# Split x kept once in DRAM: sixteen-row, four-step loads in the recurrence of a four-layer network

## What is computed

```python
xr, gate = jnp.split(x @ W_in.T, 2, axis=-1)          # inner width 1024
xr = xr + t_emb[:, None, :]
xc = silu(causal_conv4(xr, W_conv) + b_conv)
xn = (xc - mu) / jnp.sqrt(var + 1e-05) * ln_g + ln_b
Bm, Cm, dt = jnp.split(xn @ W_xproj.T, 3, axis=-1)    # 16 states
dt = jnp.tanh(dt @ W_dt.T + b_dt) * 0.01
Ad = 1.0 + dt * A
Bd = Bm * jnp.minimum(jnp.linalg.norm(xn, axis=-1, keepdims=True), 1.0)
def step(h, inputs):
    ad, bd, xt, ct = inputs
    h = jnp.clip(h * ad[:, :, None] + bd[:, :, None] * xt[:, None, :], -10.0, 10.0)
    return (h, jnp.einsum('bd,bdh->bh', ct, h))
y = ys + D * xn
out = x + y * silu(gate) @ W_out.T
```

## Time and profile before

| | us |
|---|---|
| median of 3 runs | 3763.84 (3762.84 to 3764.57) |
| the profiled execution | 3766.1, of which the span from first to last instruction is 3764.3 |
| PE busy | 3412.0 (91%) |
| DVE busy | 2965.0 (79%) |
| POOL busy | 1868.6 (50%) |
| ACT busy | 1355.2 (36%) |
| SyncE's DMA queue (q1) | 615.49 MB, 46.6% of 16 engines' time |

### The profile page before, as it was taken

One profiled execution on the slowest core, in us unless ns is written; L12 is line 12 of the kernel. 1 busy time (PEld: TensorE's weight loads), 2 busy tenths in 40 slices (PEclk: granted clock), 3 DMA queues, 4 the chain that ended last, 5 costly groups with the idle time before them and its releaser, 6 DMA issues. The chain is left out here.

```text
span 3764.3 us, 62060 instructions
## 1 busy us (share of the span) xinstructions
PE 3412.0 (91%) x22068; PEld 2260.9 (60%) x22068; DVE 2965.0 (79%) x3172; ACT 1355.2 (36%) x2078; POOL 1868.6 (50%) x1384
## 2 busy tenths in 40 slices
PE   7999839999996899999999999997999948999998
PEld 6777614444443667777777777775777733444444
DVE  4777769999996777777778777763576769999998
ACT  3555512221222553444444444432455522122121
POOL 2555645655563024444454444433355655556554
PEclk9999959999998899999999999998999968999999
DMA  4566765565554224222322222224466675555553
GB/s 128 217 259 257 271 239 203 203 219 214 200 215 142 80 72 138 85 82 78 111 96 87 80 83 85 74 63 133 162 259 237 257 294 196 217 201 210 216 206 136
DMA packets 288573, 631.00 MB, mean 168 GB/s; under 512 B 33472, under 2 KB 35904, under 8 KB 288224
## 3 DMA queue, kind: packets, MB, share of 16 engines
q1 hardware_dynamic: 281200, 615.49, 46.6%
q10 hardware_dynamic: 7104, 11.81, 0.9%
HBM read 390.75 MB, written 241.70 MB: 168 GB/s over the span
## 5 line engine op out<-in xcount | busy, mean ns | idle before, releaser
L1196 DVE CUSTOM_DVE_ANT_0 l0r_g<-l0r_g,l0r_pv,l0r_cf 128x1024 f32<-128x1024 f32 x512 | 641.9, 1336 | 20.6 <-PE l0r_pv L1005 19.0
L1196 DVE CUSTOM_DVE_ANT_0 l3r_g<-l3r_g,l3r_pv,l3r_cf 128x1024 f32<-128x1024 f32 x512 | 641.8, 1337 | 17.8 <-PE l3r_pv L1005 16.2
L137 PE MATMUL l1h_ps_p<-l1h_xh,l1c_wh 128*128 128x512 f32 x768 | 323.3, 421 | 5.6 <-issue 3.3
L139 PE MATMUL l1h_ps_p<-l1h_xl,l1c_wh 128*128 128x512 f32 x768 | 306.3, 399 | 0.0
L138 PE MATMUL l1h_ps_p<-l1h_xh,l1c_wl 128*128 128x512 f32 x768 | 304.9, 397 | 0.0
L2182 POOL TENSOR_TENSOR l1h_st<-l1h_veps 128x1 f32<-128x1 f32 x64 | 35.4, 554 | 530.5 <-DVE l1h_veps L2040 530.5
L1794 ACT ACTIVATE l1h_pt<-l1h_ps_t 128x512 f32<-128x512 f32 x256 | 151.4, 591 | 330.7 <-PE l1h_ps_t L1667 330.7
L1020 PE MATMUL l0r_py<-l0r_g,l0r_cd 128*32 128x512 f32 x2048 | 253.1, 613 | 1.3 <-ACT l0r_y L1105 1.3
L1020 PE MATMUL l3r_py<-l3r_g,l3r_cd 128*32 128x512 f32 x2048 | 252.0, 611 | 0.8 <-ACT l3r_y L1105 0.8
L2080 DVE TENSOR_TENSOR l1h_e<-l1h_e,l1h_mx 128x1024 f32<-128x1024 f32 x128 | 207.2, 1619 | 4.4
L2099 DVE TENSOR_TENSOR l1h_vt<-l1h_ps_p,l1c_dc 128x512 f32<-128x512 f32 x64 | 44.3, 691 | 194.6 <-PE l1h_ps_p L139 194.6
(11 more groups left out here) (400 smaller groups left out, 8965.1 us busy)
## 6 DMA issues: line engine op xcount, KB each, us to landing
l0r_x<-xhl_s SPq DMA_DIRECT2D x128, 512.0 KB, 5.9
l3r_x<-xhl_s SPq DMA_DIRECT2D x128, 512.0 KB, 5.7
xhl_s<-l0a_xo SPq DMA_DIRECT2D x116, 512.0 KB, 4.6
xhl_s<-l3a_xo SPq DMA_DIRECT2D x116, 512.0 KB, 4.6
gate_s<-l0a_gate SPq DMA_DIRECT2D x64, 256.0 KB, 3.0
l0r_dx<-dx_s SPq DMA_DIRECT2D x32, 512.0 KB, 7.7
l0r_gate<-gate_s SPq DMA_DIRECT2D x32, 512.0 KB, 8.6
l0r_crow<-feed_s SPq DMA_DIRECT2D x64, 256.0 KB
```

Of the source, the lines that this page charges most:

```text
L137: pe.matmul(out, wh, xh, start=first, stop=False)
L139: return pe.matmul(out, wh, xl, start=False, stop=last)
L1196: dve._custom_dve(bass.dve_ops.TENSOR_ADD_SAT, out=g[:, t, j, :], in0=g[:, (t - 1) % TS, j, :], in1=pv[(k.off + t + j) % 3][:, :], s0=cf[: ...
```

## The change

`xhl` becomes (128 steps, 64 rows, 1024): the copy `c` is gone from DRAM. Each batch's halves are stored once, by two transfers of 512 KB rather than four, on SyncE's queue and on ScalarE's. The counts that are waited for on `xo_st` are halved with them.

In the recurrence a block is loaded by eight transfers. For each of the four groups of 16 DRAM rows `r`, and for each copy `c`, one transfer brings 16 rows x four steps x 4 KB (256 KB) into 16 partitions. The 2 MB per block that reach SBUF are the same as before. All eight transfers count on one semaphore per buffer, and TensorE waits for all of them before the first step of the block, where it waited for one step at a time. At the start of the phase `load_x(1)` moves from behind `load_x(0)` to behind `load_feed(1)`.

```diff
-        x_v = dram["xhl"].rearrange("s (h a c l b) (p i) -> s c l h a b p i", h=2, a=2, c=2, l=2, p=2)
+        x_v = dram["xhl"].rearrange("s (h a l b) (p i) -> s l h a b p i", h=2, a=2, l=2, p=2)
...
             def store_batch(n):
...
-                for c in range(2):
-                    for l in range(2):
-                        sp.dma_start(x_v[:, c, l, :, n // GB % 2, n % GB, n // GB // 2, :],
-                                     xo[:, r, l, :].bitcast(F32).rearrange("s (h i) -> s h i", h=2)).then_inc(xo_st[r], 16)
+                for l in range(2):
+                    sp.dma_start(x_v[:, l, :, n // GB % 2, n % GB, n // GB // 2, :],
+                                 xo[:, r, l, :].bitcast(F32).rearrange("s (h i) -> s h i", h=2)).then_inc(xo_st[r], 16)
...
-                    at_least(act, xo_st[r], 64 * (n // 2))
+                    at_least(act, xo_st[r], 32 * (n // 2))
...
-        x_ld = ph.sems("x_ld", 2 * TS)
+        x_ld = ph.sems("x_ld", 2)
...
             def load_x(k, q):
                 at_least(sp, bmm, GJ * TS * (k - 1))
-                for t in range(TS):
-                    sp.dma_start(x[:, q, t, :, :].bitcast(F32).rearrange("p c i -> p (c i)"),
-                                 dram["xhl"][bass.ds(k * TS + t, 1), :, :].rearrange("t p i -> (t p) i")).then_inc(x_ld[TS * q + t], 16)
+                for r in range(4):
+                    rows = dram["xhl"][bass.ds(k * TS, TS), r * 2 * GB:(r + 1) * 2 * GB, :].rearrange("t p i -> p t i")
+                    for c in range(2):
+                        at = (2 * r + c) * 2 * GB
+                        sp.dma_start(x[at:at + 2 * GB, q, :, :, :].bitcast(F32).rearrange("p t c i -> p t (c i)"), rows)\
+                            .then_inc(x_ld[q], 16)
...
                         load_x(0, 0)
-                        load_x(1, 1)
                         load_tokens(0, 0)
                         store_feed()
                         load_feed(0, 0)
                         load_feed(1, 1)
+                        load_x(1, 1)
...
                 pe.wait_ge(wvm, k.count(1, 1))
+                pe.wait_ge(x_ld[k.parity()], 128 * k.uses())
                 for t in range(TS):
-                    pe.wait_ge(x_ld[TS * k.parity() + t], 16 * k.uses())
...
-    ... xhl=scratch("xhl_s", (S, P, DI)),
+    ... xhl=scratch("xhl_s", (S, P // 2, DI)),
```

More of the change, by code:

```diff
@@ L284, in store_split @@
                 sp.wait_ge((xoh, xol)[l], n + 1)
-                for c in range(2):
-                    sp.dma_start(x_v[:, c, l, :, n // GB % 2, n % GB, n // GB // 2, :],
-                                 split_rows(n)[:, l, :].bitcast(F32).rearrange("s (h i) -> s h i", h=2)).then_inc(xo_st[n % 2], 16)
+                sp.dma_start(x_v[:, l, :, n // GB % 2, n % GB, n // GB // 2, :],
+                             split_rows(n)[:, l, :].bitcast(F32).rearrange("s (h i) -> s h i", h=2)).then_inc(xo_st[n % 2], 16)
             def store_batch(n):
@@ L513, in store_high @@
                 act.wait_ge(xoh, n + 1)
-                for c in range(2):
-                    act.dma_start(x_v[:, c, 0, :, n // GB % 2, n % GB, n // GB // 2, :],
-                                  split_rows(n)[:, 0, :].bitcast(F32).rearrange("s (h i) -> s h i", h=2)).then_inc(xo_st[n % 2], 16)
+                act.dma_start(x_v[:, 0, :, n // GB % 2, n % GB, n // GB // 2, :],
+                              split_rows(n)[:, 0, :].bitcast(F32).rearrange("s (h i) -> s h i", h=2)).then_inc(xo_st[n % 2], 16)
             def halves(n):
@@ L590, in _ @@
             act.wait_ge(xol, B)
-            for c in range(2):
-                act.dma_start(x_v[:, c, 1, :, n // GB % 2, n % GB, n // GB // 2, :],
-                              split_rows(n)[:, 1, :].bitcast(F32).rearrange("s (h i) -> s h i", h=2)).then_inc(xo_st[n % 2], 16)
+            act.dma_start(x_v[:, 1, :, n // GB % 2, n % GB, n // GB // 2, :],
+                          split_rows(n)[:, 1, :].bitcast(F32).rearrange("s (h i) -> s h i", h=2)).then_inc(xo_st[n % 2], 16)
             act.wait_ge(dxm, B)
@@ L837, in _ @@
                 sp.wait_ge(g_st[r], 16 * NT * KI // 2)
-                sp.wait_ge(xo_st[r], 64 * B // 2)
+                sp.wait_ge(xo_st[r], 32 * B // 2)
                 sp.wait_ge(dx_st[r], 16 * B // 2)
@@ L912, in _ @@
             for r in range(2):
-                pool.wait_ge(sent[1][r], 64 * B // 2)
+                pool.wait_ge(sent[1][r], 32 * B // 2)
             pool.memset(cd[:, :, :, :, :], 0.0).then_inc(zeroed, 1)
@@ L2249, in scratch @@
         return nc.dram_tensor(name, shape, dt, kind="Internal").ap()
-    dram = dict(gate=scratch("gate_s", (PAIR * NBLK, GJ, TS // PAIR, GB, DI)), xhl=scratch("xhl_s", (S, P, DI)),
+    dram = dict(gate=scratch("gate_s", (PAIR * NBLK, GJ, TS // PAIR, GB, DI)), xhl=scratch("xhl_s", (S, P // 2, DI)),
                 dx=scratch("dx_s", (PAIR * NBLK, GJ, TS // PAIR, GB, DI)), feed=scratch("feed_s", (2, 2, S, 2 * P)),
```

## The result

| | before | after |
|---|---|---|
| median of 4 runs each | 3763.34 us (3762.48 to 3764.57) | 4445.41 us (4432.64 to 4464.53) |
| ratio, 95% interval | | 1.1811 (1.177 to 1.1852) |
| span of the profiled execution | 3764.3 | 4431.9 |
| first to last state update, layer 0 | 648.4 (525.8 to 1174.2) | 993.0 (520.2 to 1513.2) |
| first to last state update, layer 3 | 645.6 (3100.2 to 3745.8) | 975.7 (3437.7 to 4413.4) |

The changed kernel is slower by 18%. The forecast was 3885 us. The two recurrences lost 344.6 + 330.1 = 674.7 us, the span as a whole 667.6. The difference of 7.1 is gained outside them, 5.6 of it before layer 0's first update.

What follows compares the result with a forecast made beforehand. VectorE was taken to bound the recurrences, 20.1 us a block. Profiled 3766.1 us, plus 118 (1.9 us x 62 blocks) for the queue's excess, plus 1 for the change of phase, gave 3885 us; range 3745 to 4300.

Steps and rivals of the forecast that it cites:

- The bound: Recurrences: VectorE bounds them at 20.1 us a block while x lands in time; they can't gain from halved stores.
- The form of the sum: Recurrence block: on the feed's four engines, feed, tokens and stores, and x add in queue order, 22.0 us against 20.1.
- the turn: Recurrence: x above 10.5 us a block is the point from which the queue's excess shows.
- The term of x, 12.4 us: Recurrence block: narrow loads of x slow 2.3 times from 5.4 us; ends 5.4 and 21.6.
- The terms of the others, 5.5 + 4.1 us: Recurrence block: feed 5.5 us at 96 GB/s; dx, gate, residual and output 4.1 us at 388 GB/s.
- Rival (b): Recurrence: full crowding, x takes 21.6 us; 3950 us by landing alone, 4490 if the queue must go through; chance 0.15.
- Who waits: Recurrence: a block's first matmul waits for x, some 2 us in most blocks; GpSimd's read of dx just covered.
- The change of phase: Between projection and recurrence: halved stores and shorter waits gain 6.5 us a layer, before the late x(2).
- The barrier: Change of phase: it follows SyncE's last slow issues and comes earlier, -2.0 us a layer.
- TensorE's transposes: Change of phase: they wait for ident behind the stores; VectorE's work is next late, so -1.5 us.
- the feed stores: Change of phase: less queued ahead of them but x(0) slower, -1.0 us, ends +5 and -3.
- x(2) late: Start of recurrence: first wst delayed about 8 us, x(2) out at 552, landing 572 against 565 wanted; +7 us a layer.

Runs made afterwards that it cites:

- after_weighlate_ff: Changed kernel, with GpSimd weighing feed(k+1) only after block k-1's work and the store of block k-3 issued behind the feed; 4409.27 us, 1.1702.
- w32: Kernel before, with x loaded by four transfers of 32 neighbouring partitions x four steps and one wait for all; 3902.24 us, 1.0355.
- w64: Kernel before, with x loaded by two transfers of 64 neighbouring partitions x four steps and one wait for all; 3857.97 us, 1.0237.
- after_nofeed: Changed kernel, with no feed issued from block 2 on, so it works with stale B rows; 3817.37 us, 1.013.
- moved: Kernel before, with only load_x(1) moved behind load_feed(1); 3776.03 us, 1.003.
- w16: Kernel before, stores and start order kept, with x loaded by eight transfers of 16 neighbouring partitions and one wait; 4489.87 us, 1.1919.

## Why the prediction was wrong, step by step

**The bound.** Right for the kernel before: blocks of 20.04 us, VectorE without waits. That the recurrence can only lose by this change was right as well.

**The form of the sum.** Right. The work of a block on the four engines that carry the feed, one transfer after the other, decides. Taking the feed off (20.4 us), spreading it over sixteen engines (24), or speeding up x (20 to 22 at 210 GB/s) moved the block each time in the sense of that sum. The orders of waits and stores moved it by 4% at most (30.0 for 31.1, after_weighlate_ff), and the total by nothing clear of the noise or by 1%. The case that would have refuted it, x above 10.5 us with blocks of 20.1, did not occur, and x at 10 us (w32, w64) did sit at the turn. At 10 us the sum is 19.6, though, and blocks lasted 21 to 22: the turn is a little under 10.5.

**The term of x, 12.4 us: this step failed.** The block took 31.1 us for the 22.0 of my sum. Of these 9.1 us, x makes 3.9 (16.3 for 12.4), and the feed nearly all the rest (next paragraph). The x term was made from one row, the feed's 67 against 96 GB/s, read as 0.43 more for each further engine at the same partitions, 1 + 3 x 0.43 = 2.3. Measured are 16.3 us (after_nofeed) and 15.9 to 17.8 (2.10 MB at 132 and 118 GB/s), a factor of 388 / 132 to 388 / 118 = 2.9 to 3.3 on the tokens' rate, where I had 2.3. A slowdown of the first microseconds of a start was no measure for sixteen engines that all write into 16 neighbouring partitions. The rule of the page SBUF — State Buffer of the Trainium skill, Door 1, by its 104 GB/s, was 11% below the lowest measured rate (117), my extrapolation at 169 GB/s was 28% above the highest. I had both numbers and took the wrong one.

**The terms of the others, 5.5 + 4.1 us: these failed too.** With x at 16.3 my sum gives 25.9 us, and 31.1 were measured. The feed costs 10.6 us and not 5.5. By itself it still moves 83 GB/s, which is 6.3 us. But where its packets stand between those of x they wait as x's do. In a window of x a 4 KB packet takes an engine 1.04 x 16 / (118 / 4.096) = 0.58 us, for 0.17 at the tokens' 388 GB/s. The packets themselves bear it out: the median of the 4 KB ones is 0.56 us from 648 to 656, and 0.16 from 676 to 680, where the feed runs without x. The feed has 32 such packets on each of its four engines. All alone they would be 6.3 us, all beside x up to 18.5; the 10.6 lie between. How many stand where, I did not count. I had priced each transfer as in the kernel before, when the change altered the company they keep.

**Rival (b)** gave 31.2 us a block and 4490 us in all, and about 4400 by the Trainium skill's rate. The mechanism is the one found and its numbers are near, but not all of it held: x takes 16 to 18 us and not 21.6, and the feed makes up the difference. I had given it 0.15. What I put against it, that the feed "recovers" and that engines that get ahead spread out, no trace bears out: x stays at 118 GB/s from 648 to 656. The range, up to 4300, left the case out.

**Who waits.** Wrong. I had said that the first matmul of a block would wait for x and GpSimd's reading of `dx` would be just covered. It was GpSimd's wait for the feed that stopped the block (405.7 us), since it stands first in GpSimd's order. With that wait moved back, the ones I had named appeared (x 232.8 us, `dx` 329.4), and the time hardly changed. So I had the place wrong, and the place did not matter.

**The change of phase**, forecast at -6.5 a layer. SyncE's timeline and one row of each engine:

```profile
511.81 37.07 SPq L894 DMA_DIRECT2D l0r_wst<-L_W_outT  x8
548.93 1.13 SPq L848 DMA_DIRECT2D l0r_crow<-feed_s  x2
550.10 3.75 SPq L858 DMA_DIRECT2D l0r_x<-xhl_s  x8
```

```profile
479.15 1.76 DVE L1154 TENSOR_TENSOR l0r_g<-l0s_stat,l0s_wsum 128x1536 f32<-128x1536 f32 x1 [3.92 <-PEq L48]
```

```profile
489.38 2.79 PE L991 MATMUL l0r_pv<-l0r_ident,l0r_g 128*128 128x128 f32 x12 [19.17 <-DVE l0r_g L1164]
```

```profile
516.76 2.34 POOL L921 TENSOR_TENSOR l0r_wv<-l0r_crow,l0r_same 128x1024 fp32r<-128x1024 f32 x1 [13.05 <-DMA l0r_crow<-feed_s]
```

The barrier came at 479.15 for 484.77, -5.6 in place of -2.0. TensorE's transposes now wait for VectorE and no longer for `ident`, as forecast, but at 489.38 they are 5.9 earlier, so this gave 0.3 and not 1.5. The first weighing is at 516.76 for 522.38, again -5.6: the feed stores gained nothing net. The sum was near for layer 0, its parts were not. In layer 3 little came of it. From the last update of layer 0 to the first of layer 3 it is 1924.5 us after and 1926.0 before, and the barrier of layer 3 lies 1884.9 and 1885.6 us behind layer 0's last update.

**x(2) late: right in one number, wrong in the mechanism.** x(2) goes out at 550.10, forecast 552. I had it late for block 2, at +7 us. But I had block 2 want it at 565, and in the kernel before block 2's first update comes at 574.3. In the changed kernel x(2) has landed at 581.4 and block 2's first update comes at 583.5, with a wait for x of 1.0 us at most, since block 0 already lasted 36.8 us, 24.7 before. What made block 0 long are the output weights, as in moved. ScalarE has converted the last piece at 551.25 (544.59 before), and TensorE's read-out stops for it:

```profile
552.51 3.64 PE L1019 MATMUL l0r_py<-l0r_g,l0r_cd 128*32 128x512 f32 x16 [11.85 <-ACT l0r_y L1104]
```

At full rate I had said that the move costs nothing. It costs 12 us of recurrence in the two layers together and 9 in the median (moved). Whether it pays in the changed kernel was not run by itself. With slow loads and the old order, w16 makes its first update 31 us later than the changed kernel (551.7 for 520.2), of which some 6 are the halved stores.

**What stays open.** Why long and short blocks take turns is not explained; the mean follows from the queue, the pattern does not. A feed issued more than 12 us before x was not tried, as it needs a third buffer for the B rows or for the residual.

## What to carry to other kernels

Price a DMA by the partitions that it reaches at one moment, and not by its bytes: keep all 128 in one transfer, and put a needed copy innermost so that a row feeds two neighbours. When a queue gets near full, every other transfer in it must be priced anew at the packet time of its neighbours, and first the one that is confined to few engines. If a published rate for exactly this shape and an extrapolation from two loose rows differ, the rate carries the sum.

## What the runs showed that I had not expected

- Eight transfers of 16 neighbouring partitions in one queue, which go to different partitions one after the other, get 117 to 132 GB/s together. The page SBUF — State Buffer of the Trainium skill, section Door 1 (the DMA port swizzle), has 104 GB/s for one such transfer; in these traces transfers that follow each other in the queue add little to that.
- The busy share does not show this. It stays at 1.00 to 1.07 at 118 as at 388 GB/s; a DMA share near one says that engines are held, and only the GB/s beside it say that they move little.
- The feed's four source rows confine it to four engines (share 0.24 to 0.28). The page DMA: Bandwidth & Descriptors of the Trainium skill, section Why a DMA increments its semaphore by 16 and not by 1, says that the number of engines is the largest number up to 16 that divides the outermost sizes of both sides; with 4 source rows and 64 partitions that is 4, and the traces agree. Sixteen source rows were worth 0.3% in the kernel before, and seven tenths of the loss in the one after.
- TensorE's granted clock fell from 0.98 to 0.81 over the recurrence. It was 0.50, the lower of its two levels, from 664 to 672 us, where TensorE did nothing, and 1.00 again from 676. What this costs was not tried by itself; the changed kernel still has blocks of 20.0 us after long pauses.
